# Attention probabilities turned by VectorE and a trip through DRAM instead of by TensorE, in a two-layer fp32 kernel

## The reference

```python
q = jnp.einsum('bsd,de->bse', hidden_states, wq).reshape(B, S, H, DQ)
kv = jnp.einsum('bsd,de->bse', hidden_states, wkv)
scores = jnp.einsum('bqhd,bkhd->bhqk', q[..., :DN], k) * scale
scores = jnp.where(causal[None, None], scores, NEG_INF)
probs = jax.nn.softmax(scores, axis=-1)
attn = jnp.einsum('bhqk,bkhd->bqhd', probs, v).reshape(B, S, H * DV)
return jnp.einsum('bse,ed->bsd', attn, wo)
```

## Time and profile before

| | |
|---|---|
| median of 3 runs | 1088.01 us (1087.8 to 1088.04) |
| profiled execution, first to last instruction | 1086.1 us |
| PE busy | 1081.5 us of it |
| DVE busy | 746.5 us |
| POOL busy | 741.4 us |
| ACT busy | 561.8 us |
| granted clock of PE | 1.00 all through |

### The profile page before, as it was taken

How to read it: one execution, slowest core, us unless ns; L and a number is a source line. 1 busy time by engine, 2 the same in 40 slices (tenths; PEclk the granted TensorE clock), 3 DMA queues, 4 the chain that set the end, 5 groups by cost and what they waited for, 6 DMA issues and landing times.

```text
span 1086.1 us, 21396 instructions
## 1 busy us (share of the span) xinstructions
PE 1081.5 (100%) x6376; PEld 957.6 (88%) x6376; DVE 746.5 (69%) x1842; ACT 561.8 (52%) x1690; POOL 741.4 (68%) x1030
## 2 busy tenths in 40 slices
PE   9999999999999999999999999999999999999999
PEld 8888878998998898889888988898899889988987
DVE  7598965567767666776667666666667666676675
ACT  4445221134745555556556646654665466555663
POOL 4777567997938972977487648864795579379911
PEclk9999999999999999999999999999999999999999
DMA  5111342111200210111011101110111022001102
GB/s 174 40 59 41 105 137 68 57 37 40 79 20 20 79 40 21 40 60 39 20 59 40 39 19 59 40 39 19 60 48 49 0 60 73 25 16 57 45 1 78
DMA packets 23875, 54.39 MB, mean 50 GB/s; under 512 B 3424, under 2 KB 4000, under 8 KB 23648
## 3 DMA queue, kind: packets, MB, share of 16 engines
q1 hardware_dynamic: 23488, 52.84, 15.2%
q10 hardware_dynamic: 288, 0.52, 0.1%
HBM read 51.26 MB, written 2.10 MB: 49 GB/s over the span
## 4 chain that ended last, share of the span: by engine, by line
PE 96%; POOL 3%; DVE 1%; issue 0%; ACT 0%; POOLq 0%; DVEq 0%
PE banks L186 28%; PE banks L187 28%; PE banks L188 28%; PE banks L2074 4%; PE banks L2093 3%; PE banks L2065 3%; POOL acc L534 1%; PE banks L1315 1%; POOL form_lo L1639 0%; PE banks L1177 0%; DVE mixed L883 0%; PE banks L1365 0%; POOL form_hi L1637 0%; POOL tT_lo L540 0%; POOL wc_lo L488 0%
## 5 line engine op out<-in xcount | busy, mean ns | idle before, releaser
L1639 POOL TENSOR_TENSOR form_lo<-wqk_stage,form_hi 128x256 fp32r<-128x256 f32 x192 | 141.7, 738 | 16.0
L1693 POOL TENSOR_SCALAR vf_hi<-wvo_stage 128x512 fp32r<-128x512 f32 (+1 forms) x48 | 26.3, 547 | 168.3 <-PE banks L188 155.0
L1973 ACT ACTIVATE prob<-prob,top 128x128 f32<-128x128 f32 (+1 forms) x256 | 115.7, 460 | 15.9 <-DVE top L2002 15.7
L1979 ACT ACTIVATE prob<-prob,inv 128x128 f32<-128x128 f32 (+1 forms) x256 | 102.7, 451 | 38.5 <-DVE inv L2008 38.5
L2002 DVE CUSTOM_DVE_ANT_0 prob<-banks,mask 128x128 f32<-128x128 f32 (+1 forms) x256 | 81.3, 355 | 59.4 <-PE banks L188 46.4
L2020 DVE TENSOR_TENSOR acc<-acc,banks 128x512 f32<-128x512 f32 x129 | 86.8, 677 | 35.9 <-PE banks L188 35.7
L186 PE MATMUL banks<-tT_hi,form_hi 128*128 128x512 f32 x256 | 105.6, 412 | 0.0
L187 PE MATMUL banks<-tT_lo,form_hi 128*128 128x512 f32 x256 | 100.2, 391 | 0.0
L188 PE MATMUL banks<-tT_hi,form_lo 128*128 128x512 f32 x256 | 100.1, 391 | 0.0
L186 PE MATMUL banks<-wo_hi,oT_hi 128*128 128x512 f32 x240 | 95.9, 400 | 0.0
L188 PE MATMUL banks<-wo_hi,oT_lo 128*128 128x512 f32 x240 | 93.6, 390 | 0.0
(11 more groups left out here) (351 smaller groups left out, 3730.1 us busy)
## 6 DMA issues: line engine op xcount, KB each, us to landing
wqk_stage<-in_w_qk SPq DMA_DIRECT2D x32, 512.0 KB, 3.2
wvo_stage<-in_w_v SPq DMA_DIRECT2D x34, 256.0 KB, 2.7
wvo_stage<-in_w_o SPq DMA_DIRECT2D x32, 256.0 KB, 2.7
wd_stage<-in_w_down SPq DMA_DIRECT2D x22, 256.0 KB, 2.6
gu_stage<-in_w_gu SPq DMA_DIRECT2D x10, 512.0 KB, 3.3
out<-acc SPq DMA_DIRECT2D x7, 256.0 KB, 2.0
acc<-in_x SPq DMA_DIRECT2D x6, 256.0 KB, 6.5
tab<-in_w_comb SPq DMA_DIRECT2D x1, 1300.0 KB, 6.0
```

The lines of the kernel that those rows point to most:

```text
L1639: nc.gpsimd.tensor_tensor(form_lo[:, part], src[:, :], as_f32(form_hi[:, part]), ALU.subtract).then_inc(form_ready, 1)
L1973: ins = nc.scalar.activation(pr, pr, ACT.Exp, bias=top[:, n % 2, r:r + 1], scale=-1.0, accum_out=total[:, n % 2, r:r + 1])
L1979: ins = nc.scalar.activation(pr, pr, ACT.Copy, scale=inv[:, n % 2, r:r + 1])
```

## The change

1. 116 of the 128 pairs are no longer turned by PE. A new step Z lets DVE transpose `prob` in blocks of 32 by 32 with one instruction of 128x384 into `probT`. SP writes `probT` to DRAM (`bounce`, one DMA) and, when it has landed, reads it back with four DMAs that put each 32x32 block in its place (`pT`). A new step H copies `pT` to `pT_hi` on ACT and makes `pT_lo` on DVE. Both now read SBUF, where T's copies read PSUM. 12 pairs keep the old way: pairs 0 to 5 of the first group, 10 to 15 of the last (step T on PE, U for the copies).
2. O comes two to three pairs after its S instead of one. `pT_hi` and `pT_lo` have one buffer instead of two, and `prob` too.
3. The loop over the middle groups is written out.
4. ACT, not SP, issues the weight loads, at the new steps D and K.
5. The lists are written out step by step in a new order, and POOL's list has two tasks moved.

```diff
+MIDDLE = listed("""
+    S0 H-2 D0 X0 L0.5 K2 R0 P0.3 P1.1 Z0
+    S1 W0.0 D1 O-2 H-1 W0.1 X1 L0.3 R1 P1.6 P1.2 W0.2 Z1
...
+    S9 X9 R9 P3.1 O7 M0.3 Z9
+    S10 H8 Q1.6 E7 Q1.2 X10 R10 P3.6 K5 Z10
+    S11 M1.2 O8 H9 X11 Q1.7 Q1.4 P3.2 M1.4 L3.2 R11 W1.3 P3.7 Z11 P3.4 W1.4 L3.4 O9 H10 W1.5
...
+    S14 P4.6 X14 R14 P4.2 Z14 O12
+    S15 L4.2 P4.7 H13 X15 R15 P4.4 L4.4 Z15 O13 E13 P4.5
-        with eng.Fori(1, NG - 1) as g:
+        for g in range(1, NG - 1):
             body(g, MIDDLE)
...
+        def bounce_pair(g, steps, n):
+
+            turn = bounces(g, n)
+            sp.wait_ge(block_turned, turn + 1)
+            if landings(g, n) > 64:
+                sp.wait_ge(bounce_in[n % 2], landings(g, n) - 64)
+            sp.dma_start(bounce[n % 2], probT[:, :]).then_inc(bounce_out, 16)
+            sp.wait_ge(bounce_out, 16 * (turn + 1))
+            if g * PAIRS + n >= 2:
+                sp.wait_ge(o_done, g * PAIRS + n - 1)
+            side = P // BLOCKS
+            for c in range(BLOCKS):
+                sp.dma_start(
+                    pT[c * side:(c + 1) * side, n % 2].rearrange("j (a n) -> j a n", a=BLOCKS),
+                    bounce[n % 2][:, c * 3 * side:(c + 1) * 3 * side].rearrange("(a j) n -> j a n", a=BLOCKS),
+                ).then_inc(bounce_in[n % 2], 16)
...
     def scalar_program(act):
+        def load_qk(g, h):
+            if h >= RING:
+                act.wait_ge(form_ready, g * (GH * NP) + (h - 1) * NP)
+            act.dma_start(wqk_stage[:, h % RING], w_qk[head(g, h)]).then_inc(qk_loaded[h % RING], 16)
+
+        def load_vo(g, i, src):
+            act.wait_ge(vo_ready, pieces(g, i) - RING)
+            act.dma_start(wvo_stage[:, i % RING], src).then_inc(vo_loaded[i % RING], 16)
...
+                elif kind == "H":
+                    act.wait_ge(bounce_in[n % 2], landings(g, n))
+                    if g * PAIRS + n:
+                        act.wait_ge(o_done, g * PAIRS + n)
+                    nc.scalar.activation(by_block(pT_hi[:, :]), landed(n)[:, 0:2], ACT.Copy).then_inc(pT_hi_done, 1)
...
     def vector_program(dve):
...
+                    if is_turned(g, n - 1):
+                        dve.wait_ge(t_done, turned(g, n - 1))
+                    elif n or steps is not FIRST:
+                        dve.wait_ge(block_turned, bounces(g, n - 1) + 1)
...
+                elif kind == "Z":
+                    dve.wait_ge(norm_done, g * PAIRS + n + 1)
+                    if bounces(g, n):
+                        dve.wait_ge(bounce_out, 16 * bounces(g, n))
+                    nc.vector.transpose(probT[:, :], prob[:, :].rearrange("p (b c n) -> p c b n", b=3,
+                                                                          c=BLOCKS)).then_inc(block_turned, 1)
...
+                elif kind == "H":
+                    dve.wait_ge(pT_hi_done, g * PAIRS + n + 1)
+                    nc.vector.tensor_tensor(by_block(pT_lo[:, :]), landed(n)[:, 0:2], by_block(as_f32(pT_hi[:, :])),
+                                            ALU.subtract).then_inc(pT_ready, 1)
```

More of the change, by code:

```diff
@@ L64 @@
 LAST_MIXES = {U2: 1, C11: 2, C11_LO: 3, C12: 4, C12_LO: 5}
[L67 to L76, removed]
 AHEAD_V = range(BATCH)
@@ L119, with listed @@
[L119 to L122, removed]
+BY_DIGIT = {"1": P1, "2": P2, "3": P3, "4": P4, "5": P5, "6": P6, "7": P7}
+def listed(text):
+    steps = []
+    for word in text.split():
+        kind, rest = word[0], word[1:].split(".")
+        if kind in "PLQM":
+            steps.append((kind, int(rest[0]), BY_DIGIT[rest[1]]))
+        else:
+            steps.append((kind, *(int(n) for n in rest)))
+    return steps
@@ L123 @@
+""")
+LAST = LAST + [
     ("W", 2, NT - 1, slice(0, HALF_D)), ("W", 2, NT - 1, slice(HALF_D, DM))]
 def adds(steps):
-    return ([] if steps is FIRST else [("W", 0, 0), ("W", 0, 1)]) + [s for s in steps if s[0] == "W"]
+    return [s for s in steps if s[0] == "W"]
 def is_long(step):
@@ L143, in turns @@
     else:
-        before = [("P", 0, P7), ("W", 0, 0), ("W", 0, 1)]
+        before = [("P", 0, i) for i in (P1, P6, P7)]
     return len(before), before + [s for s in steps if s[0] in "PQW" and is_long(s) == long]
@@ L1408, in attention @@
      wvo_stage, mask) = lasting_sb
-    prob, p_full, pT_hi, pT_lo, top, total, inv, u3v = pair_sb
+    prob, probT, pT, pT_hi, pT_lo, top, total, inv, u3v = pair_sb
     HALF_G = GH * DH // 2
@@ L1446, in attention @@
     t_done = sem("t_done")
+    block_turned = sem("block_turned")
+    bounce_out = sem("bounce_out")
+    bounce_in = [sem(f"bounce_in{i}") for i in range(2)]
     pT_hi_done = sem("pT_hi_done")
@@ L1534, in turn_bank @@
         ring = LONG if long else SHORT
-        return banks[:, ring[(taken.index(step) - (len(taken) if steps is FIRST else own)) % len(ring)]]
+        at = taken.index(step) - (len(taken) if steps is FIRST else own) + (0 if long else SHORT_FROM)
+        return banks[:, ring[at % len(ring)]]
     def o_part(steps, n):
@@ new lines, in row_tiles, with bounces, same_side @@
+        yield 1, prob[:, P:3 * P], banks[:, S + p % 2, 2 * P:4 * P], mask[:, :]
+    by_vector, by_tensor = [], []
+    for g in range(NG):
+        for step in FIRST if g == 0 else LAST if g == NG - 1 else MIDDLE:
+            if step[0] == "Z":
+                by_vector.append(g * PAIRS + step[1])
+            elif step[0] == "T":
+                by_tensor.append(g * PAIRS + step[1])
+    def bounces(g, n):
+        return by_vector.index(g * PAIRS + n)
+    def same_side(g, n):
+        return [pair for pair in by_vector if pair % 2 == n % 2 and pair <= g * PAIRS + n]
@@ new lines, in landings, with is_turned, turned, by_block @@
+    def landings(g, n):
+        return 64 * len(same_side(g, n))
+    def is_turned(g, n):
+        return g * PAIRS + n in by_tensor
+    def turned(g, n):
+        return by_tensor.index(g * PAIRS + n) + 1
+    def by_block(ap):
+        return ap.rearrange("p (b a i) -> p b a i", a=BLOCKS, i=P // BLOCKS)
+    def landed(n):
+        return pT[:, n % 2].rearrange("p (a b i) -> p b a i", a=BLOCKS, b=3)
+    def second_keys(n):
+        return landed(n)[:, 2]
+    def sync_program(sp):
+        def bounce_pair(g, steps, n):
[13 more added lines that the diff above has]
+                ).then_inc(bounce_in[n % 2], 16)
+        def group(g, steps):
+            for step in steps:
+                kind, n = step[0], step[1]
+                if kind == "Z":
+                    bounce_pair(g, steps, n)
```

159 lines of the change are left out of this document (82 added, 77 removed).

## The result

The changed kernel takes 1076.02 us, the median of 3 runs (1075.64 to 1076.75), against 1088.01 before: a ratio of 0.989 with the interval 0.9874 to 0.9906. The change gained 12.0 us where the forecast had 34, and the time lies 1.0 us above the range.

A forecast was written before the change was run, and what follows sets the result against it. The prediction took PE to bound the kernel: 1088.0 - 38.3 for the transposes of 116 pairs + 4 for local crowding = 1053.7, rounded 1054 us. The range was 1047 to 1075 us.

The forecast's parts named there:

- local crowding: Slots 12 to 15 and 0 of middle groups: DVE falls 2 to 4 us behind; 4 us lost in all.
- own sign of being wrong: Waits of PE of a microsecond and more at S or at products, for DVE or ACT.
- The loop: Writing out the middle groups' loop removes 12.8 us of DVE idle time that lay behind PE; charged nothing.
- the 38.3 us: Transposes removed from PE's chain: 116 pairs at 0.33 us each.
- DVE: the sum: DVE per middle group: 71.4 + 8.0 for transposes + 7.5 for H's remainders = 86.9 of 99.3 us.
- the excess: Extra DVE time per H remainder with both inputs in SBUF: 0.47 us, up to 7.5 us per group.
- The trip: A turned pair's way from scores to O through DRAM: 10.9 us, 12.8 at the upper bound; PE does not wait.
- The slower rival: Reads from DRAM land late and ACT stands at H; PE loses 6 us per group, 1098 us; chance 0.09.
- ACT and POOL: Per middle group ACT has 60.7 of 99.3 us, POOL 27 us to spare; loads waiting in ACT's queue charged nothing.
- VectorE takes over: Rival: half of DVE's idle time stays, a middle group takes 103.5 us; 1062 to 1084 us; chance 0.27.

The follow-up runs named there:

- filler runs: Changed kernel with three matmuls issued twice in the six middle groups, in O5, O10, O13 (1078.98 us) or in O2, O7, O9 (1084.29 us).
- narrow combinations: Changed kernel with DVE's combinations and low parts kT_lo, qT_lo, v_lo on 32 columns from the second group on: 1065.18 us.
- narrow transpose: Changed kernel with 115 of the 116 DVE transposes taking only 32 of 384 columns: 1077.07 us.
- narrow remainder: Changed kernel with step H's subtraction on DVE making only 32 of 256 columns: 1075.46 us.
- two low parts earlier: Changed kernel with M1.5 moved ahead of P3.5 and M0.4 ahead of P2.4 in the middle groups: 1082.43 us.
- M1.5 alone: Changed kernel with only M1.5 (DVE's v_lo) moved ahead of P3.5 in the middle groups: 1078.7 us.
- less PE work: Changed kernel with each O of a pair turned by DVE leaving out its matmul of the third block of 128 keys: 1073.56 us.

## Why the prediction was right or wrong

**What failed is the step "local crowding":** "I expect 0 to 2 us lost per group and take 0.5: 8 x 0.5 = 4 us". It measured 2.2 to 2.8 us in the middle groups, 4.7 in each of the first two and 5.7 in the last (2.0 of them there before, too), 27.9 us in all, 26 more than without the change. Not only the size was off, the reckoning was of the wrong kind. It compared sums of busy time over 25 us of PE, where DVE would be 2 to 4 us behind, in slots 12 to 15. What PE waits for is the end of chains like the one ahead of S0, 2.4 us long with a cover of 2.0. They show in slots without crowding too (P2.5 in slot 7). The pair of filler runs shows this for the three places in the middle groups (Q1.3, P2.5, S0): a pace of DVE that is too slow as a whole would not tell O10 from O9. The narrow combinations, -10.8 us, against the narrow transpose and the narrow remainder, +1.1 and -0.6, speak for the links on DVE and against its load, but weakly: they took 174 us of busy time from DVE, the other two 36 and 22.

The moves did not bear the account out as a recipe. Of five orders made by it none was faster than the changed kernel and four were slower. It tells where PE stands; it did not tell what another order costs.

A second fault of this step is that it took the middle group for all eight. The first, second and last group have orders or neighbours of their own and lose 13.1 of the 26 us. I never laid their chains against their covers. No run tested these groups alone, so what their gaps hang on is open, except that narrow combinations took the last group's from 5.7 to 2.8 and left the second group's nearly as they were.

The prediction's own sign of being wrong did come: waits of PE of 1.0 to 1.1 us at S and at products for DVE. The loop, charged at nothing, gave 1 of the 12.0 us gained.

**PE: right.** The transposes are gone, and with them nearly the 38.3 us. With all gaps over 0.1 us taken off, the spans are 1046.0 (changed) and 1082.9 (loop written out): 36.9 us for 116 pairs, 0.32 each. The view of PE's busy time says less, 1053.9 where I wanted 1044, since short gaps count as busy in it.

**DVE: the sum was too high in one term and too low in the other.** The transpose took 0.57 us, above my bound of 0.55:

```profile
L2117 DVE STREAM_TRANSPOSE probT<-prob x116: 562/572/580, 296.1 to 1030.0; 128x384 f32<-128x384 f32 x116
...
L2125 DVE TENSOR_TENSOR pT_lo<-pT,pT_hi x116: 381/426/1421, 307.0 to 1038.1; 128x256 fp32r<-128x256 f32 x116
```

(least, median and greatest duration in ns; the second row is the remainder). The remainder's median is 0.426 us, the 0.419 of before; its mean is 0.561, so the excess is 0.14 us and not 0.47. 24 of 116 took over 0.7 us, and each of these ran beside a TENSOR_TENSOR of POOL or ran into one. One of them, ahead of an O5 that PE waited for:

```profile
608.59 0.92 DVE L2125 TENSOR_TENSOR pT_lo<-pT,pT_hi 128x256 fp32r<-128x256 f32 x1
```

```profile
608.49 0.74 POOL L1702 TENSOR_TENSOR form_lo<-wqk_stage,form_hi 128x256 fp32r<-128x256 f32 x1
609.19 0.58 POOL L1700 TENSOR_SCALAR form_hi<-wqk_stage 128x256 fp32r<-128x256 f32 x1
```

The remainder ends 0.28 us after POOL's instruction, and the next of POOL's takes 0.58 instead of 0.41. All 22 remainders that ran while POOL was idle took 0.43 us or less. By the shared pair of ports that the Trainium skill, page "SBUF — State Buffer", section "SBUF: two separate sides", describes, this is what should happen, and the trace agrees; charged to each H it was 3 times too much. On average it is small, but it falls at bad places. If one takes from each gap ahead of an O what the remainder before it took over 0.43 us, 3.6 of these 4.5 us go in the changed kernel, 7.5 of 9.3 with the two low parts earlier, 5.3 of 7.1 with M1.5 alone, 4.7 of 6.4 with narrow combinations. So most of what came back at O in the reordered kernels stands behind a remainder that POOL held up, a rival of the covers there. How much time hangs on it no run shows: the narrow remainder was held up as well, and no run moved POOL's work.

**The trip: right, within its bounds.** Write and read landed in 1.9 us (median) each, expected 2.0 and 2.3; the slowest write took 5.3. ACT's copy waited 21.3 us for the DMA in 17 places, and leaving the trip out gave 2.7 us, within the scatter. The slower rival (reads late, 1098) did not happen. The Trainium skill, page "DMA: Bandwidth & Descriptors", section "Specifications", wants at least 512 bytes per piece; the reads, 48 KB each in pieces of 384 bytes, landed after the same 1.9 us as the write of 192 KB. Whether longer pieces would land sooner no run here tests.

**ACT and POOL: right.** ACT is busy 57 us of 102, and no wait of PE hangs on its loads. POOL waits for value weights 36.5 us in 8 places and stands in no row of PE's waits; it enters them only through the remainders that it holds up.

**The rivals.** "VectorE takes over", 1062 to 1084, holds the measured time, but not with its mechanism: DVE is 79% busy in a middle group, and a VectorE that set the pace would have gained from a narrow transpose. What ends PE's waits is DVE in every row but one, yet as the last link of a chain, not as a full engine. That PE would wait at such places could have been had from the profile of before: the lengths of the links are in its rows, and the covers can be counted in the new list.

## What to carry to other kernels

When work is taken off the engine that bounds, every chain through the other engines beside which it stood loses that much cover. So before believing a sum of busy times, lay each chain (product, combination, copy, low part, next user) against the work that the new order puts beside it, in the first and last stage too. Moving one step took its own wait out here and brought others of about the same size, so a reordering has to be measured as a whole; filler work at the place tells whether a wait hangs on its own cover.

## What the runs showed of the hardware

**After some stops of 2 us and more PE's clock fell to half.** In the run with less PE work, after PE had waited 2.0 us for qT_lo (windows: length, PE busy, PEld, DVE, ACT, POOL, granted clock, DMA share, GB/s):

```profile
705.00:708.00 3.00, 1.17 (x6) 0.62 (x4) 1.76 (x7) 2.07 (x7) 2.75 (x6) 1.00 0.56 163
708.00:710.00 2.00, 1.83 (x6) 1.52 (x7) 1.22 (x4) 1.43 (x7) 1.70 (x4) 0.80 0.65 247
710.00:712.00 2.00, 1.53 (x6) 1.07 (x5) 1.57 (x4) 1.45 (x5) 1.77 (x3) 0.50 0.26 56
712.00:714.00 2.00, 2.00 (x12) 1.75 (x11) 1.63 (x3) 0.40 (x1) 0.00 (x0) 0.85 0.44 141
```

From about 709.2 to 712.7 the level is the lower of the two, 1.2 GHz, and two 512-column matmuls there start 0.43 us apart instead of 0.23. Between 708.17 and 712.72 PE did 2.4 us of work at the usual distances and stood 0.5 us, so the lower level cost some 1.6 us on top of the stop. The same followed the other two stops of over 2 us in this run (2.3 and 2.8 us). It does not follow every such stop: with the loads issued by SP, the lower level came with stops of 4.9 and 2.7 us, and not with four others of 2.0 to 3.3 us. The changed kernel's clock is full in every slice of its page.

**A DVE instruction with both inputs in SBUF was held up by POOL's TENSOR_TENSOR.** Of the changed kernel's 116 remainders (128x256) the 24 longest, 0.70 to 1.42 us, all ran beside one, 21 of them ended 0.28 us after it, and with POOL idle none took over 0.43 us. Where the remainder had started first, POOL's instruction took longer instead: ten of POOL's TENSOR_SCALARs of 128x512 (L1756) took 0.64 to 0.71 us beside one, against a median of 0.62 for all of that line and size.
